# Layernorm moved from a stage of its own into the attention block of a one-core transformer kernel

## The reference, cut to what matters

```python
x = x + attention(layernorm(x))           # 16 heads of 64, causal, masked scores = 1e-10, softmax, W_output
x = x + ffn(layernorm(x))                 # three blocks; each has two linear layers with
                                          #   w = (q / 7.5 - 1) * scale   (groups of 16) and a low-rank part
# _layernorm(x) = (x - mean) / sqrt(var + 1e-5)
# _qlora_linear(x) = x @ w.T + bias + (x @ la.T) @ lb.T
```

## Time and profile before

| | us |
|---|---|
| median of 3 runs | 2429.32 (2425.05 to 2433.47) |
| profiled execution, its own time | 2423.18 |
| its span in the trace | 2421.4 |
| TensorE busy | 2247.3 (93%) |
| VectorE busy | 1421.2 (59%) |
| GpSimd busy | 1240.8 (51%) |
| ScalarE busy | 813.6 (34%) |

### The profile page before, as it was taken

One profiled execution on the slowest core, in us unless ns is written; L12 is line 12 of the kernel. 1 busy time (PEld: TensorE's weight loads), 2 busy tenths in 40 slices (PEclk: granted clock), 3 DMA queues, 4 the chain that ended last, 5 costly groups with the idle time before them and its releaser, 6 DMA issues. The chain is left out here.

```text
span 2421.4 us, 30652 instructions
## 1 busy us (share of the span) xinstructions
PE 2247.3 (93%) x10080; PEld 1149.0 (47%) x10080; DVE 1421.2 (59%) x3782; ACT 813.6 (34%) x1166; POOL 1240.8 (51%) x1139
## 2 busy tenths in 40 slices
PE   4389999999999999999999999999999995899987
PEld 3224444444444444444444444444444442767764
DVE  3585665656665656565656565656565763265664
ACT  1113434343434343434334344434343442011111
POOL 0106666667676757575757584858584810111110
PEclk8569999999999999999999999999999998899998
DMA  4564363635354445545453536353535332521100
GB/s 122 160 157 108 83 159 80 156 95 140 102 134 111 125 122 147 130 110 134 101 140 95 151 90 152 95 147 99 147 95 141 88 93 73 193 87 61 61 18 18
DMA packets 205356, 273.61 MB, mean 113 GB/s; under 512 B 69201, under 2 KB 86801, under 8 KB 205201
## 3 DMA queue, kind: packets, MB, share of 16 engines
q1 hardware_dynamic: 205200, 271.67, 42.8%
HBM read 176.69 MB, written 94.63 MB: 112 GB/s over the span
## 5 line engine op out<-in xcount | busy, mean ns | idle before, releaser
L731 POOL TENSOR_TENSOR acc<-acc,probs 128x512 f32<-128x512 f32 (+1 forms) x900 | 980.7, 1125 | 377.6 <-ACT probs L961 377.6
L961 ACT ACTIVATE probs<-ps_s 128x1024 f32<-128x1024 f32 (+2 forms) x640 | 549.4, 897 | 332.5 <-PE ps_s L824 157.2
L1011 DVE TENSOR_REDUCE partial<-ps_bg 128x1 f32<-128x512 f32 x768 | 490.3, 684 | 202.8 <-PE ps_bg L766 202.4
L822 PE MATMUL ps_s<-qq,kk 128*128 128x512 f32 (+3 forms) x1280 | 573.2, 448 | 18.8 <-ACT probs L961 18.8
L843 PE MATMUL ps_o<-probs,v 128*64 128x512 f32 (+3 forms) x2560 | 537.8, 541 | 0.0
L824 PE MATMUL ps_s<-qm,kl 128*128 128x512 f32 (+3 forms) x1280 | 467.1, 365 | 0.0
L757 PE MATMUL ps_bg<-xs,w_in 128*128 128x512 f32 x768 | 364.5, 599 | 20.8 <-DMA xs<-xn_turned 18.9
L822 PEld LDWEIGHTS ps_s<-qq,kk 128*128 128x128 f32 x1280 | 243.5, 190 | 202.4 <-issue 154.3
L766 PE MATMUL ps_bg<-k_bf,q_bf 64*128 64x512 bf16 (+3 forms) x1280 | 274.5, 364 | 20.2 <-DVE split L988 10.4
L1008 DVE CUSTOM_DVE_ANT_0 junk<-ps_bg,mask_q 128x512 bf16<-128x512 f32 (+3 forms) x512 | 230.7, 485 | 104.7 <-issue 103.5
L843 PEld LDWEIGHTS ps_o<-probs,v 128*64 128x64 f32 x2560 | 155.3, 136 | 229.9 <-issue 206.0
(11 more groups left out here) (102 smaller groups left out, 1659.0 us busy)
## 6 DMA issues: line engine op xcount, KB each, us to landing
high_and_low<-split SPq DMA_DIRECT2D x128, 512.0 KB, 5.8
qq<-high_and_low SPq DMA_DIRECT2D x64, 512.0 KB, 4.7
kk<-high_and_low SPq DMA_DIRECT2D x128, 256.0 KB, 5.5
qm<-high_and_low SPq DMA_DIRECT2D x64, 256.0 KB, 6.4
kl<-high_and_low SPq DMA_DIRECT2D x64, 256.0 KB, 6.8
e<-masked_weights SPq DMA_DIRECT2D x128, 128.0 KB, 3.0
scale<-inverse_sums SPq DMA_DIRECT2D x128, 128.0 KB, 2.9
heads_turned<-o_out SPq DMA_DIRECT2D x64, 256.0 KB, 3.1
```

Of the source, the lines that this page charges most:

```text
L731: g.tensor_tensor(acc[h][:, group % 2, q0:q0 + w], acc[h][:, group % 2, q0:q0 + w], probs[h][:, probs_slot(i, t), at:at + w], ALU.add).the ...
L822: pe.matmul(out, kk[:, h, kb * P:(kb + 1) * P], qq[:, h, q], start=True, stop=False, skip_group_check=True)
L961: nc.scalar.activation(probs[h][:, probs_slot(i, t), 0:width], ps_s[:, h, 0:width], ACT.Exp, scale=SCORE_SCALE).then_inc(p_ready, 1)
L1011: e.reduce_max(to, of, AX.X).then_inc(max_read, 1)
```

## The change: what it does

The first stage is dropped. `load_x` loads raw rows of x into `xs` (viewed as `chunk_rows`), `row_stats` and `standardise` run on VectorE, `invert_root` on GpSimd, `turn_x` on TensorE, `take_x` on ScalarE, and the turned chunk lands in `xs`. For batch 0 this stands in the prologue, woven between the projections and through `ps_s`; for batch 1 it stands in pair 6 at the slots of `STATS_AT`, `RSTD_TILE`, `XN_AT`, `TURN_AT` and through `ps_bg`. The fill of `kl` moves from VectorE to GpSimd. Three turned values and three turned maxima of pair 0 move between its maximum units (`FIRST_FIN_AT`), the last turned maximum behind the first scores. The feed-forward weights are loaded in the last pair by 14 transfers, dequantised on GpSimd (12 instructions of 128x512), turned on TensorE at the slots of `LORA_AT` and `WEIGHT_AT`, copied by ScalarE and stored. They use tiles that are free by then (`split`, `w_in`, `xs`).

```diff
+STATS_AT = {3: 52, 2: 58, 1: 70, 0: 82}
+RSTD_TILE = {3: 10, 2: 11, 1: 13, 0: 15}
+XN_AT = {3: 70, 2: 76, 1: 88, 0: 100}
+TURN_AT = {3: 80, 2: 90, 1: 102, 0: 112}
+N_LAYERS = 6
+LORA_AT = [24 + 11 * l for l in range(N_LAYERS)]
+WEIGHT_AT = [30 + 11 * l for l in range(N_LAYERS)]
...
-FIN_FIRST = [("mt", 3), ("mt", 2), ("mt", 1), ("mt", 0), ("vt", 3), ("vt", 2), ("vt", 1)]
+FIN_FIRST = [("vt", 3), ("vt", 2), ("vt", 1), ("mt", 3), ("mt", 2), ("mt", 1), ("mt", 0)]
+FIRST_FIN_AT = [5, 8, 11, LAST_MAX[3] + 3, LAST_MAX[2] + 3, LAST_MAX[1] + 3, NMAX]
...
# SyncE
-                    sp.dma_start(xs[:, c], xnt[4 * batch + c]).then_inc(xs_loaded[c], 16)
+                    sp.dma_start(chunk_rows[c], x[4 * batch + c]).then_inc(xs_loaded[c], 16)
+                def load_ffn_weights():
+                    sp.wait_ge(proj_done, START + NPROJ * N)
+                    for b in range(2):
+                        sp.wait_ge(split_kept[b], START + 64 * N)
+                    for l in range(n_layers):
+                        sp.dma_start(w_q[l], qweights[l].rearrange("(h p) d -> p h d", p=P)).then_inc(ffn_w_loaded, 16)
+                        sp.dma_start(la_in[l], lora_a[l]).then_inc(ffn_w_loaded, 16)
+                    sp.dma_start(sc_in, w_scales.rearrange("l (h p) g -> p (l h) g", p=P)).then_inc(ffn_w_loaded, 16)
+                    sp.dma_start(lb_in, lora_b.rearrange("l (h p) r -> p (l h) r", p=P)).then_inc(ffn_w_loaded, 16)
...
                     if i:
                         store_heads(i - 1, 0)
                     if more:
                         keep_split(i + 1, 1)
                         keep_split(i + 1, 0)
+                    if not more:
+                        load_ffn_weights()
...
# GpSimd
+                def invert_root(batch, c):
+                    n = ln_count(batch, c)
+                    pool.wait_ge(var_done, START + n)
+                    g.tensor_tensor(rstd[:, n % 2], var_eps[:, n % 2], minus_half[:, :], ALU.pow).then_inc(rstd_done, 1)
+                def dequantise(l):
+                    if l == 0:
+                        pool.wait_ge(ffn_w_loaded, START + 16 * (2 * n_layers + 2))
+                    g.tensor_scalar(w_unit[l], w_q[l], 1.0 / 7.5, -1.0, ALU.mult, ALU.add).then_inc(w_units, 1)
+                    pool.wait_ge(w_units, START + l + 1)
+                    g.tensor_tensor(by_group, by_group, ..., ALU.mult).then_inc(w_dequant, 1)
...
                 masked_denominators(N - 1)
-                for c in GROUPS:
+                masked_part(N - 1, 3)
+                for l in range(n_layers):
+                    dequantise(l)
+                for c in (2, 1, 0):
                     masked_part(N - 1, c)
...
# TensorE
+                def turn_x(batch, c):
+                    n = ln_count(batch, c)
+                    pe.wait_ge(xn_done, START + n)
+                    for s in range(halves):
+                        if batch:
+                            bank_read("ln", batch, c, s)
+                            to = bank("ln", batch, c, s)
+                        else:
+                            if n >= 3:
+                                pe.wait_ge(xs_ready, START + n - 2)
+                            to = ps_s[:, n % 2, s * CH:(s + 1) * CH]
+                        for t in range(4):
+                            mm = pe.transpose(to[:, t * P:(t + 1) * P], chunk_rows[c][:, t, s * P:(s + 1) * P], ident[:, :])
+                    mm.then_inc(x_turned, 1)
+                def turn_lora(l):
+                    if l == 0:
+                        pe.wait_ge(ffn_w_loaded, START + 16 * (2 * n_layers + 2))
+                    bank_read("lora", 0, l)
...
+                def turn_weight(l):
+                    pe.wait_ge(w_dequant, START + l + 1)
+                    bank_read("weight", 0, l)
...
-                for u in range(NPROJ):
-                    project(0, u)
+                turn_x(0, 3)
+                project(0, 0)
+                turn_x(0, 2)
+                for u in (1, 2, 3):
+                    project(0, u)
+                turn_x(0, 1)
+                for u in (4, 5, 6):
+                    project(0, u)
+                turn_x(0, 0)
+                for u in range(7, NPROJ):
+                    project(0, u)
...
# VectorE
+                for c in (3, 2):
+                    row_stats(0, c)
+                    standardise(0, c)
+                dve.wait_ge(w_loaded, START + 144)
+                low(0, 0)
+                row_stats(0, 1)
+                low(0, 1)
+                standardise(0, 1)
+                low(0, 2)
+                low(0, 3)
+                row_stats(0, 0)
+                low(0, 4)
+                standardise(0, 0)
+                for u in range(5, NPROJ):
+                    low(0, u)
```

More of the change, by code:

```diff
@@ L327, in background @@
                       if at == n and pair_of(i, kind, c) < n_pairs_in_all]
-    first, users, counts = {}, [], {"proj": 0, "max": 0, "fin": 0}
+            if (i + 2) % n_pairs == 0 and i + 2 < n_pairs_in_all:
+                order += [("ln", (i + 2) // n_pairs, c) for c in PROJ_CHUNKS if TURN_AT[c] == n]
+            if i == n_pairs_in_all - 1:
+                order += [("lora", 0, l) for l in range(N_LAYERS) if LORA_AT[l] == n]
+                order += [("weight", 0, l) for l in range(N_LAYERS) if WEIGHT_AT[l] == n]
+    first, users = {}, []
+    counts = {"proj": 0, "max": 0, "fin": 0, "ln": len(PROJ_CHUNKS), "lora": 0, "weight": 0}
     for use in order:
@@ L331, in background @@
         first[use] = len(users)
-        for _ in range(2 if kind == "max" else 1):
+        for _ in range(2 if kind in ("max", "ln") else 1):
             counts[kind] += 1
@@ L469, in nth, with ln_count, xs_ready_count, next_batch @@
             return 4 * i + 3 - group
+        def ln_count(batch, c):
+            return 4 * batch + PROJ_CHUNKS.index(c) + 1
+        def xs_ready_count(batch, c):
+            done = PROJ_CHUNKS.index(c) + 1
+            return done if batch == 0 else 4 + 8 * (batch - 1) + 2 * done
+        def next_batch(i):
+            return (i + 2) // n_pairs if (i + 2) % n_pairs == 0 and i + 2 < N else None
         start_counts(nc, sems)
@@ L633, in _ @@
                         install_max(i + 1, 3)
+                    else:
+                        for l in range(4):
+                            store_ffn_weights(l)
                     spread_masked(i, 0)
@@ L645, in _ @@
                         install_chunk(i + 1, 1)
+                    else:
+                        for l in range(4, n_layers):
+                            store_ffn_weights(l)
                     take_den(i, 1)
@@ L714, in _ @@
                             masked_denominators(i)
+                        for c in PROJ_CHUNKS:
+                            if next_batch(i) is not None and t == RSTD_TILE[c]:
+                                invert_root(next_batch(i), c)
                         pool.wait_ge(p_ready, START + 2 * NT * i + 2 * t + 2)
@@ L962, in _ @@
                                                  scale=SCORE_SCALE).then_inc(p_ready, 1)
-                        if i and t == 0:
+                        if t == 0 and i == 0:
+                            evacuate(0, "mt", 0, NFIRST)
+                        elif t == 0:
                             evacuate(i - 1, "den", 0, fin_before(i, 0))
@@ L971, in _ @@
                                     evacuate(pair_of(i, kind, c), kind, c, fin_before(i, k) + 1)
+                            for c in PROJ_CHUNKS:
+                                if next_batch(i) is not None and TURN_AT[c] == n:
+                                    take_x(next_batch(i), c)
+                            for l in range(n_layers):
+                                if i == N - 1 and LORA_AT[l] == n:
+                                    take_lora(l)
+                                if i == N - 1 and WEIGHT_AT[l] == n:
+                                    take_weight(l)
                 evacuate(N - 1, "den", 0, fin_before(N - 1, NFIN))
```

364 lines of the change are left out of this document (162 added, 202 removed).

## The result

The changed kernel took 2419.2 us in the median of 9 runs (2409.15 to 2474.43), the kernel before 2428.35 in as many (2425.05 to 2447.64); the ratio is 0.9945, 95% interval [0.992, 0.9971]: some 13 us faster by the ratio and 9 by the medians, where I had forecast 33.8, and outside my range of 2374 to 2417. On two other chips the same two kernels gave 0.998 [0.995, 1.001] and 0.999 [0.9963, 1.0017], which isn't told from no change. Medians and ranges are over all runs, whereas a ratio leaves out those more than 1.5% above the fastest of their kernel (one here, two in `row_late`, one in `again_b`, six of twelve in `hold_ln` and in `pad_before`).

A forecast was written before the change was run, and what follows sets the result against it. Between the pairs only TensorE's own work was taken to count, the first 177 us being serial steps. Start -83.5, pair 6 +10 and last pair +39.7 gave -33.8 from 2429.3, so 2396 us, range 2374 to 2417.

The forecast's parts named there:

- The first stage goes; the first projections: Start: work begins at 5.2 instead of 96.87 us (-91.7); projecting the first pair with its layernorm takes 41.4, not 32.0 (+9.4).
- Maximum units and what is behind them: First pair: turns between maximum units cost +2.0, work gone behind the last unit -5.1, first scores at slow clock +1.9.
- Batch 1 in pair 6: Pair 6: transposes on TensorE 4.0, VectorE's bursts 5.0, turn 0 +1; in all +10 us (+4 to +16).
- The last pair: Weights inside the last pair: 17.3 stall, 1.8 restart, 14.2 turning, 4.4 copies, 2 dequantising; +39.7 us.
- The stall: Last pair: TensorE waits 18.4 us at its first turn for the weights' 14 transfers; net +17.3 (bounds 12 and 23).
- ScalarE's copies: Last pair: copies of turned weights push exponentials into TensorE's wait, +4.4 us (0 to +7).
- Restart: Last pair: after standing still, TensorE runs at half rate for 3.6 us of work, +1.8 us.
- GpSimd's dequantising beside VectorE's additions: Last pair: twelve dequantising steps stretch VectorE's additions, mostly absorbed by three slots of probabilities; +2 us (0 to +8).
- rival C: Last pair: port contention at its full price, +8 to +10 us, giving 2405; chance 12%.
- Rivals A: Pair 6 and last pair: the new waits hide, leaving 4.0 and 16.5 us; -63 in all, 2366; chance 13%.
- B: Start: first projections run at half rate, +19 us, giving 2415; chance 12%.
- D: Last pair: TensorE stays at half rate to its end after standing 18 us, +65 instead of +1.8; 2458; chance 3%.

The follow-up runs named there:

- row_late: Changed kernel, with GpSimd filling the row of ones in kl only after the last chunk is standardised: 2435.7 us, ratio 0.9962 to the kernel before.
- again_b: The changed kernel as it is, run once more beside the kernel before: 2438.83 us, ratio 0.999.
- hold_ln: Changed kernel, with GpSimd's additions in pair 6 waiting until a chunk of batch 1 is standardised: 2444.17 us, ratio 0.9941 to the kernel before.
- pad_before: Kernel before, with an unused tile of 336 bytes a partition, moving the large tiles by 352 bytes: 2464.96 us, ratio 1.0033 to the kernel before.
- turn_late: Changed kernel, with the weights turned 24 slots later in the last pair: 2410.3 us, ratio 0.9885 to the kernel before.
- The probe: Changed kernel preceded by 80 trains of eight GpSimd additions, each with a VectorE test instruction beside it; one execution, read by its profile, not its time.
- pad_32: Kernel before, with an unused tile of 32 bytes a partition: 2571.76 us, ratio 1.0509 to the kernel before.
- pad_384: Kernel before, with an unused tile of 384 bytes a partition: 2439.33 us, ratio 0.9983 to the kernel before.
- tiles_last: Changed kernel, with the layernorm's five small tiles allocated behind all others, restoring the old addresses: 2423.62 us, ratio 0.9925 to the kernel before.
- again: The changed kernel as it is, run again: 2433.43 us median (2412.49 to 2446.74).

## Why the prediction was wrong

**The first stage goes; the first projections (-91.7, +9.4): right but for one neighbour.** First work at 5.19 us (forecast 5.2), first projection at 18.45 (near 19). VectorE takes the first maximum at 48.78 and not at 46.6 (the 47.99 above is TensorE's first unit), so +9.4 is +11.6: the 3.4 us of the fill of one row, which I had not listed as a neighbour of the scalings, partly made good by projections that were faster than walked.

**Maximum units and what is behind them (+2.0, -5.1, +1.9): right.** From the first maximum to the first score 46.5 us instead of 48.5, at a clock of 0.53 (the earlier trace rows have 0.54): -2.0 for the three terms' -1.2. In all the first score comes 82.1 us earlier, and the first `e_sq` comes 81.3 us earlier in this pair of profiles. It varies from execution to execution: over six profiles with the old start and eight with the new it stands at 195.1 and 109.9 on average, 85.2 us apart, where 83.5 was forecast.

**Batch 1 in pair 6 (+10): failed.** "VectorE's bursts ... so each burst of 2.2 costs about 1.0" took their durations from the earlier trace rows, where GpSimd was idle. I had the meeting of the earlier trace rows in hand (2.18 us instead of 1.27), and had priced from it in the last pair only. Here the scalings of two chunks meet GpSimd's additions and take 5 us instead of 1.4: 20.5 us, and 12.4 with GpSimd held (131.03 less 118.66). The term was also added up wrongly: three bursts at 1.0 and one at 2.4 are 5.4 and not 5.0.

**The last pair (+39.7): right, but for the clock.** 43.0 measured. The stall: 18.4 forecast (17.3 net of idle time), 18.3 shown and, by turn_late, 17.8 given back. TensorE's first turn began at 1953.3, 11.6 us behind the first issue of the 14 transfers at 1941.75, where I had 11.9. No run shows the landing 5 us earlier that the lower bound of 12 takes. Turning: 14.2, and 17.6 busy us on lines 713, 725 and 729. ScalarE's copies: 4.4, and 3.0 more waiting for exponentials (4.0 against 1.0). Restart: 1.8, yet the clock fell twice (0.50 from 1953 to 1958 behind the stall; again 0.50 from 1976 to 1979, behind a gap of 1.69 us for an exponential), and the scores and weighted sums, which both kernels have, took 78.2 instead of 72.7 us: 5.5. The sum, 44.4, is within 1.4 of the whole. GpSimd's dequantising beside VectorE's additions (+2, rival C) left no visible wait: the four additions that met it took 4.28 us, the next four 2.50, so 1.8 more. No run shows the +8 to +10 of rival C. Rivals A, B and D fell too: the stall wasn't made up, the first projections ran at 1.00, and so did the last pair from 1961 to 1973.

**Starved additions: not in the sum at all.** I held the pairs that the change doesn't touch for untouched. They ran with tiles 352 bytes further on: 15 starved additions in 120 pairs, 1.9 an execution, 19 us. A third of them are in the one profile of 2472.6 us, which is longer than all other runs beside it; without it there are 10 in 105 pairs, 14 us.

Together: -83.5 + 2.2 for the start, 20.5 for pair 6, 43.0 for the end and 19 are +1 by the profiles in hand, -3 with the mean start, and with 14 in place of 19 they are -4 and -8; the medians gave -9, -7 and -2, the ratios -13, -5 and -2. How many additions starve in a run without a profile isn't known, so this last term is an estimate. The two steps that failed are one: I priced what VectorE does from rows in which GpSimd was idle or the tiles lay elsewhere. The probe shows a 32x32 addition and scalings held by one addition of GpSimd (they take 1.1 us at most), and the fill of one row shows scalings held by a GpSimd instruction that only writes (4.64 us instead of 1.38). The eight scalings of two chunks of pair 6 that each waited for one addition cost VectorE 7 us more (4.94 and 5.06 against 1.37 and 1.38). Nothing of this foretells a wait of 7.9 us over six successive additions; here the measurement decides.

## What to carry to other kernels

Here a duration held only beside the neighbours it was measured with: four scalings took 1.38 us beside an idle GpSimd and 4.64 to 5.06 beside a busy one, a cast 0.42 and 2.40, the small addition 0.18 and 1.1 or 7.9. So before a VectorE scaling, cast or two-input addition between SBUF tiles is moved, look at what GpSimd does at the new place, and count one GpSimd instruction for each (1.26 us in the probe, where these took up to 1.1). A change of layout can change every pair, as 32 bytes did (15 of 15): here new small tiles did no harm to the untouched pairs when they stood behind the old ones, nor a pad of 384 bytes, so try either, and profile more than one execution. Here a load that was issued late was cured better by a later use (17.8 us) than by an earlier place in a queue of small transfers (3.6).

## What of the hardware was not expected

- A 32x32 fp32 addition of VectorE (0.18 us alone, 1.1 when it waits for one GpSimd addition) waits 7.9 us, until a train of eight additions of GpSimd is over, when tiles are moved by 32 bytes (`pad_32`, 15 of 15 pairs), in part when by 352 bytes (`pad_before`, five of 15, and 15 of 120 in the changed kernel and its variants), and not when by 384 (`pad_384`) or 0 in the kernel before (`tiles_last`, by 0, has one of 9.16 in pair 6). The whole kernel loses 5.1% by an unused tile of 32 bytes a partition (`pad_32`, ratio 1.0509).
- Between the same two instructions at the same distance (1.46 us from the train's start in pairs 10 and 11 of the profile of 2472.6) both outcomes occur in one execution: 7.90 and 1.11 us.
- GpSimd's fill of one partition's 4,096 elements takes as long as that of 64 (3.50 and 3.51 us in `again`), and holds VectorE's scalings until it ends (4.64 us for four, 1.38 in `row_late`).
- With the first stage the first load of `e_sq` stood at 188.8 to 200.7 us, execution by execution; without it at 106.9 to 111.7, and with the edit of `row_late` at 103.9 to 104.9.
